# Windowed attention with block transposes on the vector engine, and a reordered entry of the delta layer, in a twelve-sublayer decoder on one core

## The reference

```python
x = layernorm(x + L0_ffn(x))
x = layernorm(x + L1_attn(x, w_qkvz, w_ba, conv_w, dt_bias, A_log, norm_weight, w_out))   # gated delta rule
...
x = layernorm(x + L2_attn(x, wq, wk, wv, wo))   # 16 query heads, 4 key/value heads, head size 128
# L2_attn: a query sees key k if k <= q and (k < 4 or k >= q - 31)
mask = (k <= q) & ((k < SINK) | (k >= q - WINDOW + 1))
ex = exp(where(mask, scores, floor) - rowmax) * mask
out = (ex / max(sum(ex), 1e-9)) @ v
```

## Time and profile before

| | us |
|---|---|
| median of 3 runs | 2535.57 (2530.93 to 2545.46) |
| profiled execution, its own time | 2543.06 |
| its span | 2541.3 |
| PE busy | 2146.1 (84%) |
| DVE busy | 1806.0 (71%) |
| ACT busy | 1408.6 (55%) |
| mean granted TensorE clock | 0.923 |
| delta layer | starts at about 327 |
| windowed attention | about 1528 to 1968 |

### The profile page before, as it was taken

One profiled execution on the slowest core, in us unless ns is written; L12 is line 12 of the kernel. 1 busy time (PEld: TensorE's weight loads), 2 busy tenths in 40 slices (PEclk: granted clock), 3 DMA queues, 4 the chain that ended last, 5 costly groups with the idle time before them and its releaser, 6 DMA issues. The chain is left out here.

```text
span 2541.3 us, 43026 instructions
## 1 busy us (share of the span) xinstructions
PE 2146.1 (84%) x17412; PEld 1648.2 (65%) x17412; DVE 1806.0 (71%) x3155; ACT 1408.6 (55%) x2283; POOL 200.4 (8%) x148
## 2 busy tenths in 40 slices
PE   7996477999999999999743988999999766788855
PEld 4665355777777777787732558999998533465633
DVE  4777757899888989988588353344444879678687
ACT  4654256777766777776464314455445346455346
POOL 0000101010001101001000510000000001100301
PEclk8999678999999999999876999999999877999977
DMA  3000022222222222122152551111100020000001
GB/s 151 2 1 12 3 68 69 54 65 54 59 81 67 63 55 63 51 73 59 46 190 80 126 159 62 57 17 50 37 33 1 5 79 1 11 1 2 15 1 34
DMA packets 161834, 130.62 MB, mean 51 GB/s; under 512 B 118016, under 2 KB 145280, under 8 KB 154880
## 3 DMA queue, kind: packets, MB, share of 16 engines
q1 hardware_dynamic: 158592, 123.93, 15.9%
q0 software_dynamic: 3072, 4.33, 1.0%
HBM read 106.42 MB, written 21.79 MB: 50 GB/s over the span
## 5 line engine op out<-in xcount | busy, mean ns | idle before, releaser
L1591 DVE SCALAR_TENSOR_TENSOR ctx_chan<-l1a_raw,l1a_cw,ctx_chan 128x1024 f32<-128x1024 f32 x192 | 232.1, 1280 | 19.2 <-ACT ctx_chan L1437 18.0
L1200 PE MATMUL banks<-x_chan,l1a_wp 128*128 128x512 f32 x512 | 228.3, 604 | 10.8 <-ACT l1a_vt L1487 5.7
L1200 PEld LDWEIGHTS banks<-x_chan,l1a_wp 128*128 128x128 f32 x512 | 99.1, 194 | 130.0 <-issue 123.8
L2772 PE MATMUL banks<-x_chan,more_weights_ahead 128*128 (+1 forms) x1024 | 121.1, 277 | 2.1 <-ACT l2a_ready L2628 2.1
L2772 PEld LDWEIGHTS banks<-x_chan,more_weights_ahead 128*128 128x128 f32 x1024 | 119.5, 194 | 3.8 <-issue 1.6
L1237 PE MATMUL banks<-l1a_wo,l1a_oT 128*128 128x256 f32 x512 | 117.1, 382 | 0.0
L1208 PE MATMUL banks<-l1a_wz,x_chan 128*128 128x256 f32 x512 | 114.7, 383 | 0.0
L2792 PE MATMUL banks<-l2a_wo,l2a_oT 128*128 128x256 f32 x512 | 113.2, 379 | 0.0
L1187 POOL TENSOR_TENSOR l1a_al<-l1a_aT,l1a_outer 128x1024 f32<-128x1024 f32 x32 | 74.9, 2363 | 479.9 <-DVE l1a_aT L1651 479.9
L1208 PEld LDWEIGHTS banks<-l1a_wz,x_chan 128*128 128x128 f32 x512 | 97.2, 192 | 12.8
L1237 PEld LDWEIGHTS banks<-l1a_wo,l1a_oT 128*128 128x128 f32 x512 | 96.1, 190 | 13.4
(11 more groups left out here) (628 smaller groups left out, 5609.1 us busy)
## 6 DMA issues: line engine op xcount, KB each, us to landing
l1a_sq<-l1a_norm_mem SPq DMA_DIRECT2D x16, 1024.0 KB, 4.7
ctx_tok<-l1a_rows_mem SPq DMA_DIRECT2D x16, 1024.0 KB, 8.8
ctx_chan<-in_ctxT_dram SPq DMA_DIRECT2D x3, 2048.0 KB, 18.1
l1f_wgu<-in_l1f_wgu_dram SPq DMA_DIRECT2D x4, 1408.0 KB, 11.2
moe_sums<-l1x_zero SPq DMA_DIRECT2D x2, 2176.0 KB, 17.5
ctx_tok<-in_ctx_dram SPq DMA_DIRECT2D x2, 2048.0 KB, 11.9
l1a_wp<-in_l1a_wp_dram SPq DMA_DIRECT2D x8, 512.0 KB, 5.6
l1f_wgu<-moe_sums SPq DMA_DIRECT2D x8, 512.0 KB, 7.4
```

Source lines behind the costliest of these rows:

```text
L1200: mm = MM(projected(i, u)[:, q * 512:(q + 1) * 512], wp[:, c, u * 128:(u + 1) * 128], g.xT[:, c, t0:t0 + 512], start=c == 0, stop=c == 1)
L1591: V.scalar_tensor_tensor(t, raw[:, u, :, j:j + S], cw[:, c, j:j + 1], t, ALU.mult, ALU.add).then_inc(s["conv_done" if step == 2 else "conv ...
L2772: mm = mm_(next_banks(h)[:, k, :], wq[:, c, h * HALF_HEADS + k, :], g.xT[:, c, bass.ts(i, 128)], start=c == 0, stop=c == 1)
```

## The change

**Windowed attention.** The transposes of the probabilities leave PE. DVE does them (`turn_probs`), as 32 by 32 blocks, eight heads in one instruction, and only for the nine of sixteen blocks in which the mask leaves anything (`WINDOWED`); the rest of `probsT` is cleared once at the start. DVE writes SBUF itself, so ACT's two copies per tile (L2649) go. The values product takes four heads at once, since four query heads share one key/value head: 4 products of 512 columns for 16 of 128. PE does the scores first and the next keys and values behind them.

**Delta layer.** The first weights (`wp`, `wba`, `cw`, `gates`) are held in buffers that live since the layer before last, and the sublayer ahead (`layer0_ffn`) loads them. The gate columns are formed first, with the weights (32 columns) as stationary operand on the four column tiles, 8 products of 512 columns; ACT copies the result, four transposes turn it. DVE's first gate operations stand ahead of the first convolution. The gate product z of round 0 moves from the entry into round 0, behind the projections of round 1, as in all other rounds. In round 0, silu, squares, `next_sums` and `norm_ln` of round 1 move behind the copies of `wT`.

```diff
@@ layer0_ffn, SP @@
+            sp.dma_start(g.ahead["l1a_wp"][:].rearrange("p c n -> p (c n)"), d["l1a_wp"][0]).then_inc(s["next_loaded"], 16)
...
+            sp.wait_ge(s["next_loaded"], 80)
@@ layer1_delta, PE, a round @@
-                    pe.wait_ge(s["wz_loaded"], 16 * (i // 2) + 16)
-                    for h in range(2):
...
+                pe.wait_ge(s["wz_loaded"], 16 * (i // 2) + 16)
+                for h in range(2):
+                    if more:
+                        pe.wait_ge(s["tap"], 4 * i + 7 + h)
...
+                    gate_project(i, h)
...
-                next_sums()
+                if i:
+                    next_sums()
...
+                if i == 0:
+                    next_sums()
                 solve(i)
@@ layer1_delta, PE, the entry @@
-            for u in range(2):
-                project(0, u)
-            pe.wait_ge(s["loaded"], 16 * 3)
-            for i in range(B):
-                for c in range(DC):
-                    mm = MM(ps[:, 4, i * 32:(i + 1) * 32], g.xT[:, c, i * 128:(i + 1) * 128], wba[:, c, :], start=c == 0, stop=c == 1)
+            for c in range(DC):
+                for j in range(4):
+                    mm = MM(ps[32 * j:32 * j + 32, 4, :], wba[:, c, :], g.xT[:, c, j * 512:(j + 1) * 512], start=c == 0, stop=c == 1)
             mm.then_inc(s["ba"], 1)
+            project(0, 0)
+            pe.wait_ge(s["ba_out"], 1)
+            for n in range(4):
+                mm = nc.tensor.transpose(ps[:, 5, n * 128:(n + 1) * 128], term[:, n * 128:(n + 1) * 128], g.ident[:])
+            mm.then_inc(s["ba_turned"], 1)
+            project(0, 1)
@@ layer2_attention, ACT @@
-                    act.wait_ge(s["probs_turned"], i * 2 + (h + 1))
-                    A(heads(probsT, h), half_banks(h), ACT.Copy).then_inc(s["probs_out"], 1)
@@ layer2_attention, DVE @@
+            def turn_probs(i, h):
+                v.wait_ge(s["normed"], i * 2 + (h + 1))
+                for a, b in WINDOWED:
+                    queries, keys = slice(32 * a, 32 * a + 32), slice(32 * b, 32 * b + 32)
+                    ins = V.transpose(heads(probsT, h)[keys, :, queries], heads(probs, h)[queries, :, keys])
+                ins.then_inc(s["probs_turned"], 1)
@@ layer2_attention, PE @@
-                    pe.wait_ge(s["probs_out"], i * 2 + (h + 1))
-                    for k in range(h * HALF_HEADS, (h + 1) * HALF_HEADS):
-                        mm = mm_(half_banks(h)[:, k % HALF_HEADS, :], vals[:, k // SHARE, :], probsT[:, k, :], start=True, stop=True)
+                    pe.wait_ge(s["probs_turned"], i * 2 + (h + 1))
+                    for k in range(0, HALF_HEADS, SHARE):
+                        kv = (h * HALF_HEADS + k) // SHARE
+                        mm = mm_(half_banks(h)[:, k:k + SHARE, :], vals[:, kv, :], probsT[:, kv * SHARE:(kv + 1) * SHARE, :], start=True, stop=True)
```

More of the change, by code:

```diff
@@ L1040, in projected @@
             return unit(u if i else u % 2)
-        def gate_unit(i, h):
-            return 2 + h if i else h
         def compact(n):
@@ L1501, in round_ @@
                         decay_exp(i + 1, h)
-                if i:
-                    for h in range(2):
-                        z_out(i, h)
-                    if more:
-                        for u in range(2):
-                            silu(i + 1, u)
+                for h in range(2):
+                    z_out(i, h)
+                if i and more:
+                    for u in range(2):
+                        silu(i + 1, u)
                 for h in range(2):
@@ L1510, in round_ @@
                     A(heads(ec, h), half_out(2, h), ACT.Copy).then_inc(s["e1_out"], 1)
-                if i == 0:
-                    for u in range(2):
-                        silu(1, u)
-                if more:
+                if i and more:
                     squares(i + 1)
@@ L1522, in round_ @@
                     A(heads(wT, h), half_out(2, h), ACT.Copy).then_inc(s["wT_out"], 1)
+                if i == 0:
+                    for u in range(2):
+                        silu(1, u)
+                    squares(1)
+                    norm_ln(1)
                 if more:
@@ L1611, in _ @@
             link(V.tensor_scalar(gt[0], gt[1], 1.0, None, ALU.add))
+            for step in range(3):
+                convolve(0, 0, step)
             v.wait_ge(s["gln"], 1)
@@ L2802, in step @@
                     scores(i, h)
+                if not last:
+                    project_kv(i + 1)
                 if not first:
@@ L2808, in step @@
                     project_q(i + 1, 0)
-                turn_probs(i, 0)
-                if not last:
                     if not first:
@@ L3923, in build_decoder @@
                 early.close()
+            elif sublayer is layer1_wkv:
+                delta.close()
             hold(ctx, g, sublayer)
```

105 lines of the change are left out of this document (44 added, 61 removed).

## The result

The changed kernel takes 2523.41 us (median of 10 runs, 2517.57 to 2528.10) and the kernel before, on the same chip, 2537.80 us. The ratio is 0.9943, with a 95% interval from 0.9928 to 0.9957: 14.4 us faster, where 29.6 were forecast. The profiled execution of the changed kernel has a span of 2526.0 us; that of before has 2541.3. One execution of the kernel before, taken beside the runs with seven and eleven blocks, took 6000.48 us and counts in no comparison.

What follows compares the result with a forecast made beforehand. PE was taken to bound the attention and a chain of waits the delta layer's entry; -24.6 us and -5.0 us summed to -29.6 us, giving 2506.0 us from 2535.57. The range leaving out 2 in 10 was 2498 to 2526.

Steps and rivals of the forecast that it cites:

- What bounds the kernel; PE's period: Attention: PE is the bound, with DVE over half free; the tile period falls by 1.87 us to 24.58 us.
- The chain beside PE: Attention tile, ACT and DVE: exponentials start at about 7.9 us; second half turned before PE wants it at 22.85.
- 15.2 + 18x: Attention tile: time in us after the scores start when DVE has turned the second half, x being one transpose.
- The price x: Attention, DVE: one transpose from start to start, taken as 0.33 us; the slack ends at 0.425 us.
- The estimate of 0.36 us from the Trainium skill: Attention, DVE: transpose price from two pages; second half ready at 21.7, about 0.5 us lost in the last tile.
- Rival (a): Attention: transposes of 0.42 to 0.50 us make DVE the bound; gain shrinks by some 13 us, about 2519; chance 0.14.
- rival (c): Attention tile boundary: scores wait for ACT's copy, 0.4 us late costs 6 us: 2512; chance 0.20 shared with rival (d).
- The last tile: Attention's end: transposes have no queries to hide behind; last output product 2.5 to 4.5 us later, 3.5 taken.
- Delta layer, entry: Delta layer's start: transfer wait goes, norm's last exponential ends earlier; gain 4.1 to 6.5 us, 5.0 taken.
- Rival (d): Delta layer: entry gains nothing, from low clock or later `e1`: 2511; chance 0.20 shared with rival (c).
- Round 0: Delta layer's first round: `e1` 2.8 us late, offset by moving `next_sums`; net nothing, bounds -1 and +3 us.
- e1: Delta layer, round 0: first correction's product on PE, forecast to start at about 407.4, 2.8 us late.

Runs made afterwards that it cites:

- seven blocks: The changed kernel with seven transposed blocks a half in place of nine (two that the mask needs left out): 2511.01 us.
- eleven blocks: The changed kernel with eleven transposed blocks a half in place of nine (two more, zero by the mask): 2558.35 us.
- exponentials first: The changed kernel with ACT's exponentials of heads 0 to 7 ahead of the copies of the next keys and values: 2507.36 us, ratio 0.9886.
- copies: The changed kernel with each DVE transpose made a plain copy between the same addresses: 2508.42 us.
- both joined ones: The joined kernel, 2500.39 us, and the same with round 0's gate products and z's silu back ahead of the first round, 2496.46 us.
- the joined kernel: The changed kernel with exponentials first, old order of the sums, and the last tile's probabilities turned by TensorE: 2500.39 us, ratio 0.9834.
- the old order of the sums: The changed kernel with round 0's silu, squares, sums and norm logarithm back where the kernel before had them: 2519.33 us, ratio 0.9929.

## Why the prediction was wrong, point by point

**What bounds the kernel; PE's period.** Right. Without the wait the period is 24.56 us on the mean of 14 tiles in five kernels (exponentials first, seven blocks, copies and both joined ones), 24.58 forecast.

**The chain beside PE.** Its form was right to a tenth: exponentials at 7.83 for 7.9, second half turned at 15.2 + 18x, which with x = 0.449 is 23.3; measured 1662.00 - 1638.68 = 23.32.

**The price x: the step that failed.** It was taken as 0.33 us from rows of ordinary 256-element instructions; it is 0.449. The copies show that the nearest row was near for a copy (0.298) and not for a transpose. It cost the period 0.67 us (the 0.45 us wait and 0.22 more, below), and most of the 4.1 us in the first tile, which has no output product to hide the chain and which the forecast had put down as one like the others: with copies in place of transposes the first tile is 36.43 us long for 40.69. The reasoning for 0.33 ("one read and one write per element") had nothing in the trace behind it, and the slack it left, 0.095 us a transpose, was smaller than the spread between the earlier trace rows. The earlier trace rows even have the price that was to come: the add of 256 elements (L2692) takes 0.42 us, and the next instruction starts 0.45 us behind it. The rows don't say which of the two kinds a transpose is like, and no run explains why it costs what the add costs.

The estimate of 0.36 us from the Trainium skill ("VectorE: DVE Perf Modes", The three transpose paths; "Vector Engine (DVE) Microarchitecture Reference", The reshape front-end and per-opcode configuration) doesn't come out of the figures that it names: they are 0.311 us for 128 elements a partition (in bf16), and one element a cycle for the 128 that a transpose here has more. In this kernel's rows a further element costs 1.05 ns (1.23 us for 1024 elements in a division, 0.42 for 256 in the add). If that is the cycle, the estimate is 0.311 + 0.135 = 0.45 us. The trace agrees with it (0.449 us), and it would have put the wait in the forecast.

**Rival (a)** is what happened, for transposes of 0.42 to 0.50 us. It put the loss at 13 us and the time at 2519; in the profiled executions the attention loses 16.2 us against the forecast. A chance of 0.14 was too low for a price with no row of its own next to a threshold of 0.425, with one row of its size at 0.33 us and another at 0.45.

**ACT, the tile boundary, rival (c).** Right that nothing waits there: no scores row of the changed kernel is released by `l2a_oT`.

**The last tile.** 6.15 us for 3.5. By the forecast's own terms 18 x 0.12 = 2.1 us of the 2.65 missed is x. That isn't all: with copies of 0.298 us the tail was still 4.9 us longer than before. What of this is the slow products behind the two waits and what an overlap that isn't there was not measured apart. That a page of the Trainium skill ("VectorE: DVE Perf Modes", Rules for kernel authors) sends full 128 x 128 transposes to TensorE was answered with PE's full load. The answer holds for 15 tiles and not for the last, where PE waits anyway, and there the joined kernel agrees with the page: 5.9 us less with TensorE.

**Delta layer, entry.** Right and a little low: last exponential of the norm 28.42 us into the layer for 35.36, a gain of 6.9 where 4.1 to 6.5 were given, since the gate products ran at 2.4 GHz (1.92 us). Rival (d) is out for the entry.

**Round 0: the second step that failed.** "Net nothing; bounds -1 and +3" was 5.8 us longer in the profiled execution (3.5 ahead of `e1`, where 2.8 were seen coming, and 2.3 behind it). The forecast let ACT's 7.8 us of silu, squares and norm "end at about 424.4, against 424.63 before" and took that as the end. It left out who is queued behind them: on PE the solve, whose first products stand behind the sums and so behind ACT's squares (2.73 us of waiting), and on ACT the copies of `uw`, on which the solve hangs. Before, these copies followed the norm's exponential at once too, but most of the norm's work had been done while PE still had the corrections; now it is in the open, and behind the wait PE runs at the lower clock. The exponential of the norm ends 3.0 us later after round 0's first products than before (44.86 us for 41.86), the upper bound; the other 2.8 are the solve's.

**The sum.** 24.6 + 5.0 = 29.6 us forecast; 8.35 + 1.75 = 10.1 us found in these places in one execution each, 14.4 us by the medians. Some 4 us of gain are thus in no term of the forecast (the stretch behind the last round, above, or chance). The range held the time because it had (a) in it, and even so those 4 us were luck: 10.1 us less than the 2535.57 that the forecast started from is 2525.5, at the edge of the range.

## What to carry to other kernels

A new kind of instruction whose price decides whether a second engine's chain fits under the first should be given a price from both sides, and the chance should follow from how near the threshold lies: here a transpose's 0.15 us more than a copy took 15 of the 25 us, and the trace of before already had instructions of that size at either price. Look also at what starts the chain: moving two copies of 0.6 us behind the first exponentials, with nothing made faster, gave all of it back. And when work is moved "to where the engine is idle", read the queue behind it, on that engine and on the one that waits for it: round 0's sums hid behind nothing, and the solve stood behind them on both.

## What the runs showed of the hardware

- A DVE transpose of 32 x 256 elements of f32 in 32 x 32 blocks takes 0.435 us and 0.449 from start to start; a copy between the same addresses 0.284 and 0.298, and an add of 256 elements 0.42 and 0.45. Rows of seven, nine and eleven transposes are 3.13, 4.03 and 4.93 us long, 0.449 us more for each.
- A wait of 0.45 us in PE's row of products lengthened the period by 0.67 us: from the first values product to the next scores it is 4.12 us with it (1659.81 to 1663.93) and 3.43 us without (1647.31 to 1650.74, exponentials first). With eleven blocks two breaks of 1.53 and 0.46 us lengthened it by 2.49 us. A break costs more than the idle time shown, 0.22 to 0.25 us each. Some 0.16 us of it is the tail of the last products, which lies under the next group in an unbroken row (1.88 us long, 1.72 to the next start) and lies open ahead of a break; these ends are modelled.
- TensorE went to its lower clock around waits of some 3 us inside dense work: in the changed kernel the values products behind waits of 3.16, 3.81 and 3.92 us took 2.63, 3.57 and 3.75 us for 1.96 elsewhere, those behind 2.88 us still 1.96. The length of the wait alone doesn't decide: in the kernel with the old order of the sums, products behind 2.88 and then 2.01 us took 3.75 us each. In round 0 the granted clock was 0.50 from 421 to 428 us, behind a wait of 2.73 us. In the joined kernels, with waits of at most 1.8 us in the first and the last tile, the same products ran at the upper clock.
